# Opening of an attention and feed-forward kernel: constant products first, value projections and column sums moved into other places

## The reference

```python
x = x + attn(layernorm(x), ctx, ctx)      # causal mask, Wq Wk Wv Wo with biases
x = x + ffn(layernorm(x))

# ffn: both products quantised
act_quant(x)    = round(x * 127 / max|x|) / (127 / max|x|)       # per token
weight_quant(w) = clip(round(w / mean|w|), -1, 1) * mean|w|      # per matrix
h = act_quant(x) @ weight_quant(w1).T
h = silu(depthwise_conv1d(h, conv_w, conv_b))                    # 3 taps over tokens
y = act_quant(h) @ weight_quant(w2).T
```

## Time and profile before

| | |
|---|---|
| median of three runs | 1680.63 us (1680.5 to 1683.61) |
| the profiled execution's own time | 1679.1 us |
| its span in the trace | 1677.3 us |
| busy PE / DVE / ACT / POOL | 91% / 84% / 64% / 56% of the span |
| mean granted TensorE clock | 0.97 |

### The profile page before, as it was taken

How to read it: one execution, slowest core, us unless ns; L and a number is a source line. 1 busy time by engine, 2 the same in 40 slices (tenths; PEclk the granted TensorE clock), 3 DMA queues, 4 the chain that set the end, 5 groups by cost and what they waited for, 6 DMA issues and landing times.

```text
span 1677.3 us, 24661 instructions
## 1 busy us (share of the span) xinstructions
PE 1525.8 (91%) x9198; PEld 893.0 (53%) x9198; DVE 1411.8 (84%) x2208; ACT 1067.2 (64%) x1896; POOL 939.6 (56%) x774
## 2 busy tenths in 40 slices
PE   7897998999999999999999999999999999998875
PEld 5474554646464655546464645546464655545322
DVE  7666896988979797988979797988979797977897
ACT  3456577939385765839395766849385766848362
POOL 4000446757564856757564857757564747658453
PEclk9988898999999999999999999999999999998987
DMA  8530202030210303030200303031200203020000
GB/s 248 136 121 1 64 1 64 1 91 13 48 52 1 89 1 89 1 92 14 63 32 1 89 1 89 1 92 19 62 29 7 83 1 89 1 64 1 28 25 27
DMA packets 77559, 81.00 MB, mean 48 GB/s; under 512 B 29248, under 2 KB 55104, under 8 KB 76927
## 3 DMA queue, kind: packets, MB, share of 16 engines
q1 hardware_dynamic: 77439, 79.43, 17.6%
HBM read 34.55 MB, written 19.42 MB: 32 GB/s over the span
## 4 chain that ended last, share of the span: by engine, by line
DVE 38%; issue 22%; PE 16%; ACT 13%; POOL 10%; DMA 0%; DVEq 0%; ACTq 0%; SPq 0%; POOLq 0%
DVE negm L1647 9%; DVE h L1562 8%; ACT hqb L1097 6%; DVE gall L1487 5%; POOL h L606 5%; ACT pexp L1176 4%; POOL gall L604 4%; PE ps L631 2%; DVE qhl L1608 2%; PE ps L810 2%; DVE hl L1604 2%; PE ps L804 2%; DVE xr L1694 2%; PE ps L983 2%; ACT h L1195 1%
## 5 line engine op out<-in xcount | busy, mean ns | idle before, releaser
L604 POOL TENSOR_TENSOR gall<-gall,cw 128x512 f32<-128x512 f32 x235 | 251.6, 1071 | 248.0 <-DVE h L1562 248.0
L606 POOL TENSOR_TENSOR h<-h,gall 128x512 f32<-128x512 f32 x235 | 329.9, 1404 | 18.4
L609 POOL TENSOR_TENSOR h<-h,r 128x512 f32<-128x512 f32 x240 | 306.6, 1328 | 43.8 <-DVE qb L1687 28.1
L1562 DVE SCALAR_TENSOR_TENSOR h<-gall,cw,h 128x512 f32<-128x512 f32 x256 | 258.9, 1016 | 63.3 <-ACT h L1195 63.3
L804 PEld LDWEIGHTS ps<-va,pexp 128*128 128x128 f32 x2048 | 263.1, 194 | 28.9 <-issue 9.0
L1487 DVE SCALAR_TENSOR_TENSOR gall<-ps,bias,srow 128x512 f32<-128x512 f32 x256 | 190.1, 743 | 104.4 <-PE ps L810 79.5
L810 PE MATMUL ps<-xqT,w1T 128*128 128x512 f16 x1024 | 260.9, 383 | 18.0 <-DVE gall L1487 17.3
L804 PE MATMUL ps<-va,pexp 128*128 128x33 f32 x2048 | 260.6, 272 | 0.0
L1097 ACT ACTIVATE hqb<-h 128x512 f16<-128x512 f32 x276 | 172.3, 685 | 125.9 <-PE ps L983 120.6
L983 PE MATMUL ps<-w2T,hqb 128*128 128x512 fp8e4 x960 | 242.5, 381 | 0.0
L1195 ACT ACTIVATE h<-gall,cb,cw 128x512 f32<-128x512 f32 x256 | 221.7, 866 | 8.5
(11 more groups left out here) (223 smaller groups left out, 2330.5 us busy)
## 6 DMA issues: line engine op xcount, KB each, us to landing
qs<-qhl SPq DMA_DIRECT2D x192, 128.0 KB, 2.6
xr<-in_x SPq DMA_DIRECT2D x16, 1024.0 KB, 5.5
out<-xr SPq DMA_DIRECT2D x64, 256.0 KB
h<-in_L_ffn_w SPq DMA_DIRECT2D x8, 1024.0 KB, 5.5
kst<-kh_scratch SPq DMA_DIRECT2D x32, 38.5 KB
xr<-in_ctx SPq DMA_DIRECT2D x1, 1024.0 KB
h<-in_L_xattn_Wk SPq DMA_DIRECT2D x1, 1024.0 KB, 8.3
h<-in_L_xattn_Wq SPq DMA_DIRECT2D x1, 1024.0 KB, 10.6
```

Source lines behind the costliest of these rows:

```text
L604: gp.tensor_tensor(right, right, cw[:, c, 2:3].to_broadcast([P, TB]), ALU.mult).then_inc(c2m_ok, 1)
L606: gp.tensor_tensor(hc(c), hc(c), right, ALU.add).then_inc(c2p_ok, 1)
L609: gp.tensor_tensor(hc(c), hc(c), r2[:], ALU.mult).then_inc(u_ok, 1)
L1562: ve.scalar_tensor_tensor(out=hc(c), in0=g[:, c % 4, 1:TB + 1], scalar=cw[:, c, 1:2], in1=hc(c), op0=ALU.mult, op1=ALU.add).then_inc(c1_ok, 1)
```

## The change

Six edits, all in the order or cutting of work; the only new instructions are fifteen matmuls.

1. `onesh` is filled first on POOL, and PE runs fifteen products of ones with ones into a bank that is free (`WARM = 15`) before its first transposes.
2. `v_main(0)` moves from behind `w_sums(0)` to in front of `turn_x` in slot -1; `v_main(1)` from query score 7 to in front of `w_sums(0)`.
3. `v_main(2)` is cut into thirteen single matmuls, one after each of query scores 3 to 15; `v_main(3)` alone stays behind the maxima. The values' banks and ACT's copies follow.
4. SP stores the values of batch 0 first, and waits for the values' stores and fetches them back ahead of the query DMAs.
5. In slot 0 three of four rounding and clipping steps of w2 stand ahead of the attention copies `at_high` and `at_low`, and the fourth behind them (before, all four roundings stood ahead and all four clippings behind).
6. `w2_colsums` becomes `w2_colsum(n)`, one matmul after each of the sixteen query scores of slot 1.

```diff
@@ sync engine, slot -1
                     fetch_k(0)
                     load_x(1, 1)
                     sp.wait_ge(su_kvh, 2 * NG + 1)
+                    store_v(0)
+                    sp.wait_ge(su_kvh, 2 * NG + 2)
                     store_v(-1)
+                    sp.wait_ge(v_out[0], 64)
+                    sp.wait_ge(v_out[1], 16)
+                    fetch_v(0)
...
                 if s == -1:
-                    sp.wait_ge(su_kvh, 2 * NG + 2)
-                    store_v(0)
-                    sp.wait_ge(v_out[0], 64)
-                    sp.wait_ge(v_out[1], 16)
-                    fetch_v(0)
                     sp.wait_ge(su_kvh, 2 * NG + 3)
                     store_v(1)
@@ tensor engine
-            pe.wait_ge(const_ok, 2)
+            pe.wait_ge(const_ok, 1)
+            for _ in range(WARM):
+                mm(F[0], onesh[:, 0:P], onesh[:], start=True, stop=True)
+            pe.wait_ge(const_ok, 3)
...
-            def w2_colsums():
-
-                pe.wait_ge(w_out, 2 * CT)
-                pe.wait_ge(x2_ok, at(1, TT, TT))
-                for c in range(CT):
-                    r = mm(F[1][0:1, :], onesh[:, 0:1], w2T[:, c, :], start=c == 0, stop=c == CT - 1)
-                r.then_inc(w_cs, 1)
+            def w2_colsum(c):
+
+                if c == 0:
+                    pe.wait_ge(x2_ok, at(1, TT, TT))
+                pe.wait_ge(w_out, CT + c + 1)
+                r = mm(F[1][0:1, :], onesh[:, 0:1], w2T[:, c, :], start=c == 0, stop=c == CT - 1)
+                if c == CT - 1:
+                    r.then_inc(w_cs, 1)
...
+                    if s == -1 and c == LASTU + 2:
+                        v_main(0)
                     if do_q and c == LASTU + 2:
                         turn_x(range(KT))
...
                 if s == -1:
+                    v_main(1)
                     w_sums(0)
-                    v_main(0)
...
-                    if s == -1 and n == 7:
-                        v_main(1)
-                    if s == 1 and n == 4:
-                        w2_colsums()
+                    if s == -1 and n >= 3:
+                        v_main(2, (n - 3,))
+                    if s == 1:
+                        w2_colsum(n)
...
                 if s == -1:
-                    v_main(2)
                     v_main(3)
@@ scalar engine
                 if s == 0:
-                    for i in range(KT):
+                    for i in range(KT - 1):
                         w_round(1, i)
                 if do_a:
                     for k in range(NG):
                         at_high(k)
+                if s == 0:
+                    w_round(1, KT - 1)
...
                 if s == -1:
-                    v_copy(0)
-                    w_round(0, 0)
-                    w_round(0, 1)
                     v_copy(1)
-                    w_round(0, 2)
-                    w_round(0, 3)
+                    for i in range(KT):
+                        w_round(0, i)
@@ vector engine
+                if s == 0:
+                    for i in range(KT - 1):
+                        w_limit(1, i)
                 if do_a:
                     for k in range(NG):
                         at_low(k)
                 if s == 0:
-                    for i in range(KT):
-                        w_limit(1, i)
+                    w_limit(1, KT - 1)
```

More of the change, by code:

```diff
@@ L369, in build @@
         TURNS = 2 * KT + 4 * KT
+        WARM = 15
         def turns_ahead(u):
@@ L543, in _ @@
             gp = nc.gpsimd
+            gp.memset(onesh[:], 1.0).then_inc(const_ok, 1)
             gp.memset(identf[:], 0.0).then_inc(const_ok, 1)
-            pool.wait_ge(const_ok, 1)
+            pool.wait_ge(const_ok, 2)
             gp.affine_select(out=identf[:], in_=identf[:], compare_op=ALU.not_equal, fill=1.0, base=0,
@@ L554, in _ @@
             gp.memset(negh[:], -HALF).then_inc(const_ok, 1)
-            gp.memset(onesh[:], 1.0).then_inc(const_ok, 1)
             gp.memset(mhalf[:], -0.5).then_inc(const_ok, 1)
@@ L692, in v_tails, with v_main @@
                     for bb in range(NBATCH):
-                        mm(A[4][bb * HD:bb * HD + S1, :], ctxT[:, c, i, bb * S + P:(bb + 1) * S], WvT[:, a, i, :],
+                        mm(A[5][bb * HD:bb * HD + S1, :], ctxT[:, c, i, bb * S + P:(bb + 1) * S], WvT[:, a, i, :],
                            start=n == 0, stop=False, tile_position=(0, bb * HD))
                 for bb in range(NBATCH):
-                    r = mm(A[4][bb * HD:bb * HD + S1, :], onesh[0:2, 0:S1], kvrow[:, 1, :], start=False, stop=True,
+                    r = mm(A[5][bb * HD:bb * HD + S1, :], onesh[0:2, 0:S1], kvrow[:, 1, :], start=False, stop=True,
                            tile_position=(0, bb * HD))
                 r.then_inc(su_kv, 1)
-            def v_main(b):
-                if b >= 1:
+            def v_main(b, ns=range(len(V_TERMS) + 1)):
+                bank = A[4 + (b == 2)]
+                if b >= 1 and ns[0] == 0:
                     pe.wait_ge(su_kvh, 2 * NG + b)
-                terms = [(ctxT[:, c, i, b * S:b * S + P], WvT[:, a, i, :]) for i, a, c in V_TERMS]
-                terms.append((onesh[0:2, 0:P], kvrow[:, 1, :]))
-                split_products(A[4 + (b + 1) % 2], terms).then_inc(su_kv, 1)
+                for n in ns:
+                    if n < len(V_TERMS):
+                        i, a, c = V_TERMS[n]
+                        mm(bank, ctxT[:, c, i, b * S:b * S + P], WvT[:, a, i, :], start=n == 0, stop=False)
+                    else:
+                        mm(bank, onesh[0:2, 0:P], kvrow[:, 1, :], start=False, stop=True).then_inc(su_kv, 1)
             def w_sums(w):
@@ L1128, in v_copy @@
             def v_copy(b):
-                n = b + 1
-                act.wait_ge(su_kv, 2 * NG + n + 1)
+                bank = A[5] if b in (-1, 2) else A[4]
+                act.wait_ge(su_kv, 2 * NG + (2 if b < 0 else 1 if b == 0 else b + 2))
                 if b < 0:
@@ L1136, in v_copy @@
                 for rows in (slice(bb * HD, bb * HD + S1) for bb in range(NBATCH)) if b < 0 else (slice(0, P),):
-                    r = copy(vsb[rows, V_AT[n], :], A[4 + n % 2][rows, :], scale=1.0 / WS)
+                    r = copy(vsb[rows, V_AT[b + 1], :], bank[rows, :], scale=1.0 / WS)
                 r.then_inc(su_kvh, 1)
@@ L1261, in slot @@
                             normalise1(2 * (u - 6))
+                    v_copy(0)
                 if s == 0:
```

## The result

The changed kernel took 1669.24 us (median of 13 runs, 1665.43 to 1681.66) against 1680.67 for the kernel before (13 runs, 1673.93 to 1696.22); the ratio is 0.9946, 95% interval 0.9926 to 0.9965. The forecast was 1669.6. When I timed the same kernel again later, the ratio was 0.999 (0.9973 to 1.0007), and the two intervals do not overlap. Both results stand. Over both sets together the changed kernel has a mean of 1674.0 us (25 runs) and the kernel before one of 1679.1 (42 runs), which is about 5 us, half of the gain that was forecast. Much of what follows is about how the two sets fit together.

The account below looks back on a forecast made before the run. No single engine bounds the kernel, but whichever wait ends last in each stretch. Gains of 0.7 + 8.4 + 0 + 1.9 = 11.0 us from 1680.6 gave 1669.6, range 1665 to 1676.

Parts of the forecast that it names:

- A: Fifteen constant products before the opening's transposes: first key product earlier through the clock, gain 0.7 us, bounds 0 and 2.4.
- B: `v_main(0)` ahead of `turn_x` in slot -1: fills PE's wait, `turn_x` at the upper clock, value -0.4 us.
- C: `v_main(1)` ahead of `w_sums(0)` in slot -1: DVE's first maximum at 68.3 instead of 69.82, 1.5 us gained.
- D: Single matmuls among slot -1's rough scores: DVE's 2.47 us wait goes, cost 0.2, maxima take 12.2 us.
- E: One value block instead of two behind slot -1's maxima: first score at 84.0 instead of 92.41.
- SP's queue: Query DMAs behind the value stores before slot 0: landed by 81, 3 us ahead of the score, cost 0.
- F: Slot 0's rounding and clipping in new order: worth 0 us, bounds -0.5 and +0.5.
- G: Column sums singly in slot 1: maxima 3.5 us earlier, `negmT` later, gain 1.9 us, bounds 0 and 3.9.
- R3: Slot 0's scores stay at the lower clock longer and take the gain back: about 1680 us, chance 0.08.
- R1: Upper clock holds from the constant products through DVE's wait in the opening: gain 12.7 us, 1668, chance 0.15.
- R2: Another wait takes the place in slot -1 or slot 2: gain about 5 us, 1675.5, chance 0.12.
- R4: Whole slot-0 score loop at the lower clock: 18 us lost against 11 gained, 1687, chance 0.05.

Follow-up runs that it names:

- after_again: The changed kernel, unaltered, timed a second time beside the kernel before: 1677.16 us, ratio 0.999.
- xq_early: The changed kernel with the copy of the column sums behind the first two `xqT` copies in slot 1: 1672.17 us, ratio 0.998.
- values_only: The kernel before with only the value products, their copies and SP's stores in the new places: 1677.92 us, ratio 0.9997.
- clip_only: The kernel before with only slot 0's first three roundings and clippings ahead of the split output: 1678.17 us against 1675.80, ratio 1.0008.
- colsums_only: The kernel before with only one column sum behind each rough score of slot 1: 1678.76 us, ratio 1.0002.

## Why the prediction was right, and where it was not

**Time.** 1669.6 was forecast, 1669.24 measured, and the profiled execution came out at 1669.01 against 1668.1. By the second timing the forecast would have been 7.6 us too low, and outside its range. So the hit to 0.4 us was luck: the first set was a favourable draw, and the mean of all 25 runs is 1674.0, 4.4 above the forecast. In the first trace, too, errors cancelled: A brought 1.2 more than forecast, and slot 0 took 1.5 that stood in no term.

**A, the products: 0.7 forecast, 1.9 in the first trace.** The step that failed is "PE would then wait for DVE at 14.66 all the same; DVE's list is not changed". The list is not changed, but its first instruction lasts 1 or 8 us by a contest with POOL that no row of the old trace priced. In the first trace it came out short, and 0.9 of the 1.9 us is that; the rest is faster transposes. Where it came out long (after_again, xq_early) the step holds to the letter, PE starts again at 14.66 and 14.64, and A is worth nothing: 24.92 and 24.87 against 24.89. So the length of one instruction had been taken from one execution as if it belonged to the instruction.

**B, `v_main(0)` ahead of `turn_x`: −0.4 forecast, −0.6 measured at the start of the queries' projection** (52.08 against 53.42, less A's 1.9), and for the reason given. `turn_x` took 1.97 us instead of 3.39. All nine traces with the product in PE's gap have the clock at 1.00 there, and four of the five without have 3.4 us at 0.50. The window of after, against 0.57 for the same one of before:

```profile
47.00:51.00 4.00, 4.00 (x53) 2.66 (x56) 2.52 (x5) 2.65 (x5) 0.00 (x0) 1.00 0.17 31
```

**C and D.** The times that the forecast gives for B to E leave A out. The first maximum came at 66.42, 1.9 us earlier than its 68.3, and that is A's 1.9: C was right. The sixteen maxima took 12.0 us, forecast 12.2: one product's pieces do fit beside each maximum. **E** came out at 82.55, where 84.0 less A's 1.9 is 82.1, so it was 0.5 us late. The block ran at the upper clock as assumed, and the landing of `m_in` ends the wait, as forecast, but from the turning of the maxima to the score it took 4.1 us and not 3.4, of which 0.4 is the landing (2.6 us, forecast 2.2). B to E alone are 7.9 in the first trace and 8.1 without products (values_only); forecast 8.4.

**SP's queue** was said to have 3 us of room, and had none: `store_v(1)` ended at 79.65, and the maxima's DMA was issued at 79.70. Its two stores and the landing between 59.6 and 66.6 took 7 us, where I had counted 4.7. The copy of the maxima ended at 79.45, so the queue cost about 0.2 us. In the nine traces the room between the end of that store and the maxima's DMA was 0.05 to 1.1 us.

**F: 0, and 0 was measured** (clip_only: the time and the stretch are the same within their noise). **G: 1.9 forecast, 2.1 in after,** 3.5 gained by the maxima and 1.4 given back behind the sums' copy; 1.0 of it is had by moving the copy (xq_early). Alone it brought 1.4 (colsums_only).

**The rivals.** R3 has come nearest to what happened: slot 0's scores stay longer at the lower clock. I gave it 0.08 as a case that eats everything. It is not a case but a term, 0 to 9 us with a mean of 3.5, and it belonged in the sum. Its price, 20/46 of a us for each us at the lower clock, was right (0.46 by the traces). The forecast's own sign for it, slot 0 over 4 us longer from its first score to slot 1, was not met in the changed kernel (93.4 and 96.0 us, 92.2 before), but in four of its variants (96.8 to 100.8 us). R1 needed the clock to hold from the products through the transposes; it fell between 9.7 and 13.6 in every trace with products. R2's waits took under 2 us. R4 was not seen in a trace: the longest low time in the stretch was 34.1 us, 17 more than before and short of the 25 from which it decides. But values_only had a run of 1687.62 us at a mean clock of 0.961, which is about 30 us more at the lower clock than the trace before has.

**The bounds.** Two sums of the forecast's range do not come out: the low end of the gain is 4.8 and not 4.7, and the high end, with A, G, F and B at their best, is 15.3 and not 14.4. The range as stated, 4.6 to 15.6, holds both.

## What to carry to other kernels

Price a stretch that is moved earlier at both clock levels, and the stretch behind it too: here the opening gave 8 to 11 us in every trace, and the score loop behind it took back up to 9. When an engine's first instruction takes much longer than the same instruction elsewhere (8.17 against 1.14 us here), look at what the neighbour does at that moment; one wait on POOL made it 0.95 us in five traces of five. And one timing of 13 runs, with a tight interval, showed 11 us of gain where the next showed 1: where a kernel's runs fall into groups by the mean clock, time it in more than one set, and compare traces stage by stage rather than medians.

## What the hardware showed that was not expected

- A VectorE instruction of 0.95 us was held for 8.0 to 8.2 us while GpSimd filled buffers back to back, in seven of nine traces, and ended 0.8 us after the last fill. In one where it was not held, a fill on GpSimd took 1.03 us instead of 0.23.
- TensorE was granted 0.50 with 100% of the time busy, in stretches whose length differed from one execution to the next: between S0 and the first output product 13.7 to 34.1 us in fourteen traces, each us costing 0.4 to 0.5.
- The granted clock is shown as 1.00 from the start in kernels without constant products, though the first context transposes take 0.45 us there and 0.30 with them.
